# Copies of the next pair's queries issued at a pair's first step, and VectorE's row maxima ahead of its low parts in the second pass

## What is computed

```
xn = layernorm(x)
q  = rmsnorm(xn @ q_a) @ q_b           # 32 heads, 128 plain + 64 rotated
kv = rmsnorm(xn @ kv_a[:, :64]) @ kv_b # keys 128, values 128 per head
k_pe = rope(xn @ kv_a[:, 64:])         # 64, shared by the heads
idx = sum_n iw_n * relu(iq_n @ ik.T)   # 16 indexer heads
mask = causal & top128(idx)            # per query row
attn = softmax(where(mask, (q_nope @ k_nope.T + rope(q_pe) @ k_pe.T) * s, -inf))
x + (attn @ v) @ o_w + experts(xn)
```

## Time and profile before

| | |
|---|---|
| median of 3 runs | 929.11 us (928.5 to 930.42) |
| profiled execution, its own time | 927.43 us |
| its span | 925.6 us |
| TensorE matmul busy | 808.1 us, 87% |
| VectorE busy | 674.0 us, 73% |
| ScalarE busy | 601.8 us, 65% |
| GpSimd busy | 532.0 us, 57% |
| row maxima, L1237 | x256, 191.5 us |
| score matmuls, L701 | x1152, 231.1 us |

### The profile page before, as it was taken

How to read it: one execution, slowest core, us unless ns; L and a number is a source line. 1 busy time by engine, 2 the same in 40 slices (tenths; PEclk the granted TensorE clock), 3 DMA queues, 4 the chain that set the end, 5 groups by cost and what they waited for, 6 DMA issues and landing times.

```text
span 925.6 us, 20231 instructions
## 1 busy us (share of the span) xinstructions
PE 808.1 (87%) x7496; PEld 500.8 (54%) x7496; DVE 674.0 (73%) x1557; ACT 601.8 (65%) x1340; POOL 532.0 (57%) x440
## 2 busy tenths in 40 slices
PE   4979989987768898898888898999999988989998
PEld 2435544444435555565555566666666666664443
DVE  5365678799999999999998777777877777760000
ACT  2656789979886788787887666666766666650000
POOL 3184278877874545545554777777877767650000
PEclk9989999989999999999999999999999999999999
DMA  7012211203443444443542678767576776771211
GB/s 246 24 35 80 80 35 47 85 12 100 121 111 92 136 118 115 124 124 106 140 121 58 109 137 138 139 141 141 121 138 125 120 143 139 150 141 28 69 53 38
DMA packets 168787, 96.67 MB, mean 104 GB/s; under 512 B 116721, under 2 KB 142705, under 8 KB 168689
## 3 DMA queue, kind: packets, MB, share of 16 engines
q1 hardware_dynamic: 168688, 95.37, 44.1%
HBM read 36.62 MB, written 6.29 MB: 46 GB/s over the span
## 4 chain that ended last, share of the span: by engine, by line
PE 46%; DVE 25%; issue 12%; POOL 7%; ACT 7%; DMA 2%; SPq 1%; DVEq 0%; POOLq 0%; ACTq 0%
PE psS L701 12%; PE psS L774 9%; DVE arena L1237 6%; DVE arena L1043 5%; PE psT L758 5%; DVE m L1177 5%; ACT arena L805 4%; DVE bias L1184 4%; PE psT L553 3%; PE psT L573 2%; PE psS L530 2%; POOL arena L1351 2%; PE psO L728 2%; PE psS L586 2%; DVE bias L1128 2%
## 5 line engine op out<-in xcount | busy, mean ns | idle before, releaser
L701 PE MATMUL psS<-keyT,arena 128*128 128x512 f16 (+3 forms) x1152 | 231.1, 329 | 33.0 <-issue 17.9
L992 ACT ACTIVATE arena<-arena,small 128x512 f32<-128x512 f32 (+7 forms) x256 | 198.2, 774 | 70.4 <-DVE small L1242 38.2
L805 ACT ACTIVATE arena<-psT 128x512 f16<-128x512 f32 (+4 forms) x360 | 171.8, 505 | 97.1 <-PE psT L622 43.8
L1043 DVE SCALAR_TENSOR_TENSOR arena<-psT,arena 128x512 f16<-128x512 f32 (+3 forms) x278 | 146.7, 547 | 97.4 <-ACT arena L805 96.6
L1237 DVE CUSTOM_DVE_ANT_0 arena<-psS,bias 128x512 f32<-128x512 f32 (+7 forms) x256 | 191.5, 748 | 1.0 <-PE psS L701 0.6
L701 PEld LDWEIGHTS psS<-keyT,arena 128*128 128x128 f16 x1152 | 91.5, 98 | 89.7 <-issue 23.2
L758 PE MATMUL psT<-ident,arena 128*128 128x128 f32 x736 | 115.6, 278 | 26.8 <-DVE arena L1043 23.9
L586 PE MATMUL psS<-ikT,big 128*128 128x512 f16 (+3 forms) x528 | 104.4, 343 | 22.9 <-DVE bias L1128 19.4
L758 PEld LDWEIGHTS psT<-ident,arena 128*128 128x128 f32 x736 | 84.4, 141 | 60.1 <-ACT arena L992 32.8
L1417 POOL TENSOR_TENSOR bias<-arena,bias 128x768 f32<-128x768 f32 (+2 forms) x48 | 91.4, 1919 | 32.9 <-ACT arena L871 21.7
L1184 DVE MATCH_REPLACE8 bias<-m,bias 128x768 f32<-128x768 f32 (+4 forms) x112 | 89.9, 809 | 0.0
(11 more groups left out here) (164 smaller groups left out, 1382.4 us busy)
## 6 DMA issues: line engine op xcount, KB each, us to landing
arena<-arena SPq DMA_DIRECT2D x192, 128.0 KB, 2.4
arena<-in_wiq SPq DMA_DIRECT2D x32, 256.0 KB, 2.7
arena<-in_ow SPq DMA_DIRECT2D x16, 512.0 KB, 3.5
arena<-in_qbT SPq DMA_DIRECT2D x16, 256.0 KB, 2.5
wvo_parts<-arena SPq DMA_DIRECT2D x16, 256.0 KB, 2.0
arena<-in_qpe SPq DMA_DIRECT2D x16, 128.0 KB, 2.9
arena<-in_x SPq DMA_DIRECT2D x8, 256.0 KB, 3.0
out<-arena SPq DMA_DIRECT2D x8, 256.0 KB, 2.0
```

The costliest lines, as they stand in the source:

```text
L701: last = mm(bank[:, k:k + w], Q[:, u % 2, h, a, q:q + P], keyT[:, b, h, k:k + w], start=(a, b) == (0, 0), stop=(a, b) == (1, 0))
L805: return nc.scalar.activation(dst, src, ACT.Copy, scale=scale)
L992: nc.scalar.activation(pr[:, g % 4, 0:kw], pr[:, g % 4, 0:kw], ACT.Exp, bias=shift[:, g % 4:g % 4 + 1], scale=-1.0, accum_out=rsum[:, unit ...
L1043: return v.scalar_tensor_tensor(out=dst, in0=src, scalar=scale, in1=hi, op0=ALU.mult, op1=ALU.subtract)
```

## The change

Three edits, in the order of the work alone; no instruction is added or removed.

- SyncE: `place` for the next unit, both halves, moves to the unit's first step, ahead of the transposing DMA of step 1. It stood behind that DMA.
- GpSimd: `rope_low` for the next unit goes ahead of the row parts of step 1.
- VectorE: in the second pass `row_max(g + 3)` goes ahead of the low parts, of `ot_low` and of `q_raw` of step g. In the first pass it stays behind them.

```
--- before.py
+++ after.py
@@ -465,12 +465,11 @@
             load_ow(0)
             for g in range(STEPS):
                 u, s = divmod(g, 8)
+                if s == 0 and 2 <= u + 1 < NU:
+                    place(u + 1, latent, qa_lo, q_lat, 1)
+                    place(u + 1, turned, q_rot, q_tur, 0)
                 if turns(g):
                     turn(g)
-                if s == 1 and 2 <= u + 1 < NU:
-                    place(u + 1, latent, qa_lo, q_lat, 1)
-                if s == 2 and 2 <= u + 1 < NU:
-                    place(u + 1, turned, q_rot, q_tur, 0)
                 if s == 3 and u + 2 < NU:
                     swap(u + 2)
                 if s == 4 and u + 1 < NP:
@@ -1288,11 +1287,21 @@
                 else:
                     top_mark(t, i % 2, found[t])
 
+            def next_max(g):
+                if g == 8 * NP:
+                    for t in GROUPS[2]:
+                        mask(t)
+                    dve.wait_ge(mask_done, 7)
+                if g < STEPS:
+                    row_max(g)
+
             for g in range(AHEAD):
                 row_max(g)
             dve.wait_ge(eps_ok, 2)
             for g in range(STEPS):
                 u, s = divmod(g, 8)
+                if half_of(g):
+                    next_max(g + AHEAD)
                 for use in uses_of(g):
                     what, at, c = use
                     if what == "T":
@@ -1301,12 +1310,8 @@
                         ot_low(psT[BANK[use]], at)
                     elif what in ("R", "L") and half_of(g):
                         q_raw(psT[BANK[use]], what, at)
-                if g + AHEAD < STEPS:
-                    if g + AHEAD == 8 * NP:
-                        for t in GROUPS[2]:
-                            mask(t)
-                        dve.wait_ge(mask_done, 7)
-                    row_max(g + AHEAD)
+                if not half_of(g):
+                    next_max(g + AHEAD)
                 if s == 4 and u:
                     unit_out(u - 1)
                 for i in MARK_STEPS.get(g, ()):
@@ -1485,10 +1490,10 @@
 
             for x in range(STEPS):
                 u, s = divmod(x, 8)
+                if s == 0 and 2 <= u + 1 < NU:
+                    rope_low(u + 1)
                 if x + 1 < STEPS and turns(x + 1):
                     rows_lo_(x + 1)
-                if s == 0 and 2 <= u + 1 < NU:
-                    rope_low(u + 1)
                 if s == 3 and u + 2 < NU:
                     rope_cos(u + 2)
                 if s == 5 and u + 2 < NU:
```

## The result

The changed kernel takes 898.21 us, median of 4 runs (895.79 to 899.01), against 928.87 us for the kernel before (928.5 to 930.42, now of four runs). The medians differ by 30.7 us, 3.3%; the ratio taken over the runs is 0.9656, with a 95% interval of 0.9637 to 0.9676. The forecast was 903.1 us and its range 899.5 to 914; the kernel came out faster than the whole range, by 1.3 us.

The account below looks back on a forecast made before the run. TensorE was taken to bound the second pass, with only its idle time to gain; -15.9 - 11.9 + 3 - 1.7 = -26.5, rounded to -26, gave 901.4 us profiled, 903.1 us as median; range 899.5 to 914.

Parts of the forecast that it names:

- Rival A: Step-1 transpose, now behind the copies, makes TensorE wait before the values matmuls; 1 us a unit, 918 us; chance 0.13.
- Rival C: Unit starts: copies come no earlier, as the low part waits for ScalarE's rounding; no change, 929 us; chance 0.04.
- B: Low parts free transposes' banks late, at output transposes and next projections; 0.7 us a unit, not 0.2; 910.6 us; chance 0.15.
- all there is to gain is its idle time: Second pass: TensorE is the bound, its idle time the whole possible gain, 23.9 + 3.5 + 3.0 = 30.4 us.
- 898.7 us as the floor: Whole kernel's time if all TensorE idle time of the second pass's three stretches, 30.4 us, went.
- 15.9 for the copies: Unit starts: query copies issued at the first step land with 3 us margin, so all twelve waits go, -15.9 us.
- 11.9 for the maxima: Fourth and eighth score blocks: maxima ahead of low parts, so 33 TensorE waits go, -11.9 us.
- the give-back: Output transposes: low parts start only after the step-1 maxima, 0.2 us a unit of a possible 0.5, +3 us.
- the end of the pass: Last maxima no longer wait for low parts; waits of 1.7 and 0.5 us mostly go, -1.7 us.
- in time: Three of the pass's fifteen changes of unit, where the copies were read as landing before the next scores.
- small waits that I can't see: Reason for rounding the summed gain from -26.5 to -26 us.
- D: Step-5 maxima wait for GpSimd's step-1 row parts, holding low parts; loss from +17.4, 938 us at +18; chance 0.05.

Follow-up runs that it names:

- sp_only: Kernel before with SyncE's new order alone; GpSimd still makes the low part after the row parts of step 1: 911.22 us, ratio 0.9804.
- pool_only: Kernel before with GpSimd's new order alone; SyncE still issues the step-1 transpose ahead of the copies: 956.34 us, ratio 1.0291.
- change_again: The changed kernel itself once more, beside the kernel before on one chip: 896.78 us, ratio 0.9662.
- maxima_only: Kernel before with VectorE's new order alone, copies and rotated low part where they were: 924.79 us, ratio 0.9947.
- turn_before_place: Kernel before with VectorE's and GpSimd's new orders, SyncE's old one (step-1 transpose issued ahead of the copies): 956.45 us, ratio 1.03.
- pool_late1_recip: Changed kernel plus one 1.38 us GpSimd write ahead of step-1 row parts, second-pass unit_out product replaced by a reciprocal: 909.32 us, ratio 0.9785.
- maxima_at_odd: Changed kernel, but VectorE's maxima go ahead only on odd steps: 922.12 us, ratio 0.9931.

## Why the prediction was wrong

**What held.** TensorE is the bound of the second pass and its waits were what there was to gain; the copies' lateness was SyncE's order, as sp_only and pool_only show from both sides; the ladder of one unit came out within 0.4 us at each step (low part ends at +10.6 forecast, +10.9 measured; row parts +13.9, +14.1; transpose issued at +14.0, +14.15; end of the step-5 wait +14.2, +14.2). Rival A did not come: no values matmul waits for a transpose in the change (one does in change_again, 0.2 us), and the transposes land after 3.4 to 6.3 us, where they took 3.4 to 5.9. The Trainium skill's rule on completion order (DMA: Bandwidth & Descriptors, Queues, rings and completion order) is not contradicted, but it had no price here. In 11 of the 15 units the last copy lands up to 2.8 us after the transpose of step 1 is issued, and that transpose then lands 4.3 to 6.3 us after its issue, 5.0 in the mean, against 4.3 to 6.0 and 4.8 before. Rival C did not come. B was half there: its place and its releaser were right, and the size, 0.36 us a unit, lies between the forecast's 0.2 and its 0.7.

**The step that failed** is one under the whole sum: "all there is to gain is its idle time", and with it 898.7 us as the floor. So both of its large terms, 15.9 for the copies and 11.9 for the maxima, were sized too small; they measured 18.7 and, less the give-back, 10.8 for 8.9. The rows' idle time is not the whole price of a wait. From one score block's start to the next the same work takes:

```
                               before    change   idle in the rows of before
seventh to eighth block        1.97      1.50     0.31
third to fourth                2.22      2.05     0.36
eighth to the next unit        2.40      2.18     0.05, too short to be listed
                               3.51      2.18     1.15
                               4.14      2.18     1.79
```

In the last three lines 0.17 to 0.18 us are lost beyond the idle time, in the first 0.16 (in the second the give-back hides it). It is so in other kernels, too: at all fifteen unit starts of the kernel before, maxima_only, pool_only and turn_before_place the time lost is the idle time and 0.16 or 0.17 us, for waits of 0.05 to 4.08 us. The three unit starts that I read as "in time" had waits of 0.05, 0.11 and 0.05 us, below the 0.15 at which the listing begins, and lost 0.22 to 0.28. The rows count the surplus as busy: the same matmuls of the fourteen units are busy for 264.31 us before and 260.42 after.

The rows also suggest what it is. In an unbroken run of the kernel before a matmul lasts 0.38 us and the next starts 0.22 us after it:

```profile
653.70 0.38 PE L618 MATMUL psT<-qlT,w1hi 128*128 128x512 f16 x1
653.92 0.38 PE L619 MATMUL psT<-qlT,w1hi 128*128 128x512 f16 x1
654.13 0.38 PE L620 MATMUL psT<-qlT,w1lo 128*128 128x512 f16 x1
```

Each overlaps the one before by 0.16 to 0.17 us. Idle time counts from the end of the last matmul, and a matmul that waits loses this overlap as well. The sizes agree; that it is nothing else, no run shows, since the ends of matmuls are modelled.

Summed over the second pass by start-to-start times, the gain is:

```
fifteen unit starts, 51.34 - 32.65                     18.7   (forecast 15.9)
eighth block, 15 x 0.47                                 7.0   } forecast 11.9
fourth block, 14 x 0.17                                 2.4   } less 3
rest of the pass's first unit, 20.53 - 2.1 - 17.05      1.4   }
rest of the end of the pass, 23.04 - 21.41 - 0.47       1.2   (forecast 1.7)
small differences elsewhere                             0.4
                                                       31.1
```

The copies' term was mis-sized by 2.8 us: 0.17 us at each of the twelve waits, and the three starts that looked free. The maxima's term was 11.9 - 3 = 8.9 and measured 10.8. Its two halves both moved: the waits were worth more (0.47 for 0.31), and the give-back at the output transposes, which I took at 0.2 us of a possible 0.5, measured 0.36, from 0.53 (0.36 of idle and 0.17) to 0.17. Of this 0.36, 0.14 are the idle time before L736 and 0.17 the overlap. I also rounded half a microsecond away for "small waits that I can't see"; what I couldn't see had the other sign. One row I misread without effect: L1442 ends 5.0 us into the next unit, not 4.7.

The range had a fault of its own. The floor worked out as 898.7 stood in the text, the range began at 899.5, above it, and no case lay below the floor, though it had one source only, an idle column.

**D** had the right mechanism and the wrong distance. I put its beginning at +15.4 against a forecast of +13.9, 1.5 us of room. Added work of 1.38 us already cost 12 us and 2.8 us cost 38, which by a straight line between them gives a loss against the kernel before from about 2.4 us on; the forecast said 3.5. The room is smaller since held maxima hold low parts and projections too, as the timeline of pool_late1_recip shows, and not only the score bank: with one write only 3.0 of the 12 us are lost at the eighth block. It happens in the change itself once in a while, in change_again at 658.82:

```profile
655.45 1.65 POOL L1469 TENSOR_TENSOR arena<-arena 128x768 f16<-128x768 f32 x1
...
657.14 0.82 DVE L1236 CUSTOM_DVE_ANT_0 arena<-psS,bias 128x640 f32<-128x640 f32 x1 [1.46 <-POOL arena L1469]
...
658.82 0.39 PE L617 MATMUL psT<-qlT,w1hi 128*128 128x512 f16 x1 [0.71 <-DVE arena L1042]
```

That the copies and the maxima are not additive (21.5 apart, 30.7 together) was in neither forecast nor rivals; the sum treated them as independent. It came near for the pair only because both gates were opened at once: with the maxima's alone, the unit starts grew from 51.3 to 57.6 us. To that extent it was luck.

## What to carry to other kernels

A wait on a saturated engine can cost more than the idle time in its rows: compare start-to-start times of the same block with and without the wait, and let no floor rest on the idle column. A listing of waits has a least length, so look for gaps below it, too. Where two gates hold one engine, try them together before judging either: here one alone gave 4.8 us, one third of the change alone lost 27, and all of it won 31. When a variant is slower than its waits explain, look at the granted clock: of those 27 us about 10 were the clock. Moving independent work ahead of waiting work is free only while the moved work itself never waits; a producer (here GpSimd) that runs 1.4 us later is then paid for by everything behind.

## What I had not expected of the hardware

A VectorE product of 128x8, 0.17 us long, took up to 1.29 us, 0.97 or more as a rule, when it started while a GpSimd product was running, and ended 0.02 to 0.03 us behind that one; with one tensor input (128x4) it was held just the same. In three units of maxima_at_odd it started first, by 0.02 to 0.10 us, and took 0.17. A reciprocal of the same size, inside the same GpSimd instructions, took 0.18 to 0.20 us every time, and the maxima and low parts with one operand in PSUM were never stretched. The Trainium skill (SBUF — State Buffer, Who interferes with whom) says that a VectorE instruction with two SBUF inputs contends with a GpSimd instruction that reads SBUF, and of VectorE's two-port modes, which `tensor_scalar` can enter, that whoever issues first gets the shared ports for the whole instruction while the other is blocked. The traces agree for the product, down to the end times and the order of starts, and show that 0.17 us of work is enough to be caught; in which mode the one-input product ran, no row shows.

The second was the price of a restart: 0.16 to 0.17 us beyond each wait of TensorE, the same behind 0.05 us of waiting as behind 4.08.
